# Expert stages of a hybrid layer stack: routing of the first part inside the stage ahead, and top-1 results scattered home

## The reference

```python
def _L0_ffn_ref(x, W1, b1, W2, b2, Wr, br):      # top-1: W1 (8, 128, 512), W2 (8, 512, 128)
    logits = x @ Wr + br
    idx = jnp.argmax(logits, axis=-1)
    probs = jax.nn.softmax(logits, axis=-1)
    gates = jnp.take_along_axis(probs, idx[..., None], axis=-1)[..., 0]
    ...
    for ei in range(e):
        h = jax.nn.gelu(xf @ W1[ei] + b1[ei], approximate=False)
        y = h @ W2[ei] + b2[ei]
        mask = (idxf == ei).astype(xf.dtype)
        out = out + y * (gf * mask)[:, None]

def _L1_ffn_ref(x, gate, W1, b1, W2, b2):        # top-2: W1 (8, 128, 256), W2 (8, 256, 128)
    raw_gate = jax.nn.softmax(jnp.einsum('btd,de->bte', x, gate), axis=-1)
    topk_scores, topk_idx = jax.lax.top_k(raw_gate, TOP_K)
    ...
    gate_topk = gate_topk / jnp.maximum(gate_topk.sum(axis=-1, keepdims=True), 1e-12)
    h = jax.nn.relu(jnp.einsum('btd,edh->beth', x, W1) + b1[None, :, None, :])
    expert_out = jnp.einsum('beth,ehd->betd', h, W2) + b2[None, :, None, :]
    out = jnp.einsum('bte,betd->btd', gate_topk, expert_out)
```

## Time and profile before

| | us |
|---|---|
| median of 3 runs | 2268.59 (2267.01 to 2269.56) |
| profiled execution | 2265.75 |
| its span | 2264.0 |
| stage boundaries in it | 154.1, 331.3, 847.9, 1020.5, 1167.4, 1374.6, 2060.1 |

### The profile page before, as it was taken

How to read it: one execution, slowest core, us unless ns; L and a number is a source line. 1 busy time by engine, 2 the same in 40 slices (tenths; PEclk the granted TensorE clock), 3 DMA queues, 4 the chain that set the end, 5 groups by cost and what they waited for, 6 DMA issues and landing times. The chain is left out here.

```text
span 2264.0 us, 28290 instructions
## 1 busy us (share of the span) xinstructions
PE 1647.6 (73%) x8402; PEld 974.4 (43%) x8402; DVE 1665.7 (74%) x3318; ACT 1054.8 (47%) x2009; POOL 1049.0 (46%) x845
## 2 busy tenths in 40 slices
PE   5636935899999985945635943887988888885692
PEld 2326931233333325943435941443443443343692
DVE  7985546888888825546766662899999999997664
ACT  3433640566666771626832632534434444431361
POOL 5636331222222005352207771567666666574776
PEclk8656966999999995977765976988987997896696
DMA  8012315333333201212002530000000000000363
GB/s 248 1 6 69 86 35 63 40 43 45 44 41 44 32 2 46 83 55 61 0 1 76 163 104 33 0 1 1 1 1 0 0 1 0 0 0 12 101 167 107
DMA packets 141594, 102.53 MB, mean 45 GB/s; under 512 B 16360, under 2 KB 133360, under 8 KB 141328
## 3 DMA queue, kind: packets, MB, share of 16 engines
q1 hardware_dynamic: 129168, 75.72, 15.9%
q0 software_dynamic: 12288, 25.19, 3.8%
HBM read 42.92 MB, written 38.27 MB: 36 GB/s over the span
## 5 line engine op out<-in xcount | busy, mean ns | idle before, releaser
L1520 POOL TENSOR_TENSOR m_hc<-m_state,bc 128x512 f32<-128x512 f32 x256 | 378.2, 1477 | 216.9 <-DVE m_state L1463 216.9
L931 DVE TENSOR_REDUCE maxima<-banks 128x1 f32<-128x512 f32 x512 | 320.2, 681 | 46.9 <-PE banks L781 45.8
L1390 ACT ACTIVATE banks<-banks,rates 128x512 f32<-128x512 f32 x256 | 168.8, 661 | 342.7 <-PE banks L1236 342.2
L889 ACT ACTIVATE h_p<-banks 128x512 f32<-128x512 f32 x512 | 274.0, 597 | 113.6 <-PE banks L789 112.5
L1463 DVE TENSOR_TENSOR_SCAN m_state<-banks,m_drive 128x512 f32<-128x512 f32 x256 | 310.1, 1212 | 22.9 <-ACT banks L1390 20.4
L533 POOL DMA_INDIRECT yg<-sorted_y,index x192 | 194.6, 1014 | 171.3 <-DMA sorted_y<-ys 105.3
L329 ACT ACTIVATE hid<-banks,slot 128x128 f32<-128x128 f32 x708 | 211.4, 367 | 110.1 <-PE banks L285 109.8
L522 POOL DMA_INDIRECT sorted_x<-xn,index x192 | 195.1, 1016 | 90.0 <-issue 57.1
L781 PE MATMUL banks<-ks,qs 128*128 128x512 bf16 x512 | 204.8, 402 | 40.8 <-DMA qs<-nothing 22.5
L285 PE MATMUL banks<-xt,slot 128*128 128x128 f32 x1416 | 212.4, 286 | 11.7 <-DVE slot L459 9.8
L293 PE MATMUL banks<-slot,hid 128*128 128x128 f32 x1416 | 201.1, 276 | 0.0
(11 more groups left out here) (253 smaller groups left out, 3030.6 us busy)
## 6 DMA issues: line engine op xcount, KB each, us to landing
xg<-sorted_x SPq DMA_DIRECT2D x58, 256.0 KB
sorted_y<-ys SPq DMA_DIRECT2D x58, 256.0 KB
qs<-part SPq DMA_DIRECT2D x144, 64.0 KB
ks<-part SPq DMA_DIRECT2D x144, 64.0 KB
sorted_x<-zeros SPq DMA_DIRECT2D x3, 1984.0 KB, 15.6
t1w<-in_t1w SPq DMA_DIRECT2D x16, 256.0 KB, 5.9
sorted_x<-xn,index POOLq DMA_INDIRECT x192, 2.2
yg<-sorted_y,index POOLq DMA_INDIRECT x192
```

The costliest lines, as they stand in the source:

```text
L889: act.activation(f.p[:, slot % 2, j, :], m.bank[5 + item % SHIFTED_BANKS][:, :], ACT.Exp, scale=1.0 / math.sqrt(HD)).then_inc(f.exps, 1)
L931: dve.reduce_max(f.maxima[:, tile, head:head + 1], m.bank[bank][:, :], AX_X).then_inc(f.ring_read, 1)
L1520: pool.tensor_tensor(f.hc[:, n % 8, :], f.state[:, n % 4, :], f.bc[:, now[1] % 2, 1, :], ALU.mult).then_inc(f.weighed, 1)
```

## The change

- Routing of part 0 of every expert stage is done inside the last rounds of the stage ahead, in generators that are run forward at given slots of those rounds (`front.until(...)`). It has buffers of its own (`front1...`, `front2...`). After its drain POOL scatters part 0 ahead of the barrier. DVE's slots in HEADS' last round are 0, 2, 8, 10 and 11 (statistics, normalising, choice, gates, places), in MAMBA's last full round 1, 4, 16, 20 and 26; in RWKV and LAPLACE they stand at the ends of the last rounds.
- Routing of the later parts is done inside the group loop, on PE and ACT ahead of the group that `FRONT_AT` names, on DVE two groups earlier; ranks and places are later by `RANKS_AT`. POOL's order is now [scatter(0)], rstd(1), scatter(1), rstd(2), scatter(2), then the way back.
- The top-1 stages take 3 and 5 batches. A sorted row has 129 floats, the last of them the token's number. Rows that no token fills carry a number behind the tokens'; they are written at the start by four DMAs from `pads`, which ACT fills. A result row goes home by its own number (`send_back`, one indirect DMA per group, 46 where there were 32 gathers), SP fetches each batch with a plain load, and the additions of part 0 stand six groups ahead of the loop's end. ACT's fills ahead of HEADS wait for all results kept.
- At the start POOL has two iotas more, ACT the fill of `pads` ahead of `decay`, and SP's constant loads wait for it. HEADS_GAP is 250 instead of 3392, a semaphore of HEADS is merged into another, and buffers are allocated in another order.

```diff
-PARTS = {1: (4, 4), 2: (2, 3, 3)}
+PARTS = {1: (3, 5), 2: (2, 3, 3)}
+ROW = P + 1
+EARLY_ADDS = 6
-HEADS_GAP = 3392
+HEADS_GAP = 250
+RANKS_AT = {1: 4, 2: 0}
+FRONT_AT = {1: (None, 0), 2: (None, 0, 4)}
...
+def front_vector(dve, m, f, at):
+    f.tally = Tally(dve, f.steps, f.base.steps)
+    yield at[0]
+    part_statistics(dve, m, f, f.parts[0])
+    yield at[1]
+    normalise_part(dve, m, f, 0)
+    yield at[2]
+    f.arrive(dve)
+    choose(dve, m, f, 0)
+    yield at[3]
+    gates(dve, m, f, 0)
+    yield at[4]
+    places(dve, m, f, 0)
...
 def sorted_tensor(pe, nc, m, s, f, stage):
...
     for g, (c, t) in enumerate(f.groups):
+        for p in range(1, len(f.parts)):
+            at = FRONT_AT[f.top][p]
+            if g == at:
+                pe.wait_ge(f.kept, f.base.kept + max(at - 2, 0))
+                tokens(p)
+            if g == at + RANKS_AT[f.top]:
+                pe.wait_ge(f.kept, f.base.kept + max(g - 2, 0))
+                ranks(pe, m, f, p)
...
+        if g == 0:
+            turn_sorted(0)
         if t == 0 and c + 1 < len(f.chunks):
             turn_sorted(c + 1)
         first_layer(g)
...
 def sorted_scalar(act, nc, m, s, f, stage):
...
     if f.fill:
-        act.wait_ge(f.second, f.base.second + len(f.groups))
+        act.wait_ge(f.kept, f.base.kept + len(f.groups))
...
 def sorted_vector(dve, nc, m, s, f, stage, last_stage):
...
-    statistics(f.parts[0])
-    normalise_part(0, f.parts[0])
-    for p, part in enumerate(f.parts):
-        if p + 1 < len(f.parts):
-            statistics(f.parts[p + 1])
-        route(p, part)
-        places(p, part)
-        if p + 1 < len(f.parts):
-            normalise_part(p + 1, f.parts[p + 1])
...
+    for g in range(len(f.groups)):
+        for p in range(1, len(f.parts)):
+            if g == max(FRONT_AT[K][p] - 2, 0):
+                part_statistics(dve, m, f, f.parts[p])
+                normalise_part(dve, m, f, p)
+                choose(dve, m, f, p)
+                gates(dve, m, f, p)
+            if g == max(FRONT_AT[K][p] + RANKS_AT[K] - 2, 0):
+                places(dve, m, f, p)
+        more = g + 4 < len(f.groups)
+        if more:
+            expert = expert_of(g + 4)
+        keep(g)
+        if more:
+            fill_slot(g + 4, expert)
+        if f.back and g == len(f.groups) - EARLY_ADDS:
+            add_part(f.parts[0])
...
 def sorted_pool(pool, nc, m, s, f, stage):
...
+    def send_back(g):
+        c, t = f.groups[g]
+        pool.wait_ge(f.noted, f.base.noted + c + 1)
+        pool.wait_ge(f.kept, f.base.kept + g + 1)
+        pool.indirect_dma_start(m.home[:, :], bass.IndirectOffsetOnAxis(ap=f.home[:, g:g + 1], axis=0),
+                                f.ys[:, g, :], None).then_inc(f.scattered[f.chunks[c].p], 16)
+
+    for p in range(1, len(f.parts)):
+        inverse_deviations(pool, m, f, p)
+        scatter(pool, f, p)
+    if f.back:
+        for g in range(len(f.groups)):
+            send_back(g)
...
 def sorted_sync(sp, nc, m, s, f):
...
+    def fetch(p, b):
+        sp.wait_ge(f.scattered[p], f.base.scattered[p] + 16 * (f.parts[p].lanes + f.parts[p].groups))
...
+        sp.dma_start(f.yg[:, b * TILES:(b + 1) * TILES, :], m.home[b * S:(b + 1) * S, :].rearrange("(t p) d -> p t d", p=P)).then_inc(f.stored[b % 3], 16)
...
+    front = Beside(front_vector(dve, m, f.ahead, (0, 2, 8, 10, 11)))
...
+    front = Beside(front_vector(dve, m, f.ahead, (1, 4, 16, 20, 26)))
...
-            sp.wait_ge(s.filled, 1)
+            sp.wait_ge(s.filled, 2)
...
             act.wait_ge(s.filled, 1)
+            act.activation(m.pads[:, :, 0:P], m.zeros[:, :].unsqueeze(1).to_broadcast([P, sum(back), P]), ACT.Copy).then_inc(s.filled, 1)
...
-                between(pool, n)
+                if n + 1 < len(stages) and stages[n + 1] in (TOP1, TOP2):
+                    pool.drain().then_inc(s.stage, 1)
+                    f.ahead.arrive(pool)
+                    scatter(pool, f.ahead, 0)
+                    pool.wait_ge(s.stage, 4 * (n + 1))
+                else:
+                    between(pool, n)
```

More of the change, by code:

```diff
@@ L477, in add, with add_part @@
         last.then_inc(f.added, 1)
[L479 to L497 removed]
+    def add_part(part):
         for b in part.batches:
@@ L563, in sorted_sync @@
             load(c + 3)
-        store(c)
+        if not f.back:
+            store(c)
+    if f.back:
+        for p, part in enumerate(f.parts):
+            for b in part.batches:
+                fetch(p, b)
 def experts_pool(pool, nc, m, s, f, stage):
@@ L596, in body @@
             last.then_inc(f.out, 1)
+        if now and not new:
+            pe.wait_ge(f.k_kept, BATCHES)
+            front.until(0)
+        if late and not now:
+            front.until(1)
     rounds(pe, body, 4)
@@ L637, in rwkv_vector @@
     u = f.first[:, :]
+    front = Beside(front_vector(dve, m, f.ahead, (0, 2, 3, 3, 3)))
     def body(new, now, late, done):
+        ending = late and not now
         if late:
@@ L683, in body @@
             dve.scalar_tensor_tensor(f.rw[:, :], f.num[:, :], 0.5, f.inverse[:, :], ALU.mult, ALU.mult).then_inc(f.mixed, 1)
+        if now and not new:
+            front.until(0)
+        if ending:
+            front.until(3)
     rounds(dve, body, 4)
@@ L706, in body @@
             normalise(pool, nc, m, s, ahead, stage)
+        if late and not now:
+            inverse_deviations(pool, m, f.ahead, 0)
     rounds(pool, body, 4)
@@ L853, in body @@
                 turn_maxima(now, 0)
+            if former and not now:
+                front.until(slot)
         if former:
@@ L1093, in body @@
             last.then_inc(f.out, 1)
+        if now and not new:
+            pe.wait_ge(f.queries, BATCHES)
+            pe.wait_ge(f.values_biased, BATCHES)
+            front.until(0)
+        if late and not now:
+            front.until(1)
     rounds(pe, body, 4)
@@ L1134, in laplace_vector @@
     ahead = Steps(dve, f.ahead_steps, 3)
+    front = Beside(front_vector(dve, m, f.ahead, (0, 1, 2, 2, 3)))
     def body(new, now, late, done):
+        if late and not now:
+            front.until(1)
         if done:
@@ L1189, in body @@
             dve.tensor_scalar(size, size, TINY, 8.0, ALU.max, ALU.min).then_inc(f.sizes, 1)
+        if now and not new:
+            front.until(0)
+        if late and not now:
+            front.until(2)
+        if done and not late:
+            front.until(3)
     rounds(dve, body, 4)
@@ L1393, in body @@
                 beside.until(n)
+            if now and not new:
+                front.until(n)
     rounds(act, body)
```

514 lines of the change are left out of this document (320 added, 194 removed).

## The result

| | before | after |
|---|---|---|
| median of 4 runs, us | 2267.8 (2265.82 to 2269.56) | 2338.86 (2335.64 to 2341.98) |
| profiled execution, its span | 2265.75, 2264.0 | 2340.35, 2338.2 |
| RWKV | 154.1 | 173.8 |
| first top-1 stage | 177.2 | 168.2 |
| HEADS | 516.6 | 515.4 |

The changed kernel is slower: ratio 1.0313, 95% interval 1.0295 to 1.0331. The forecast was slower, 2300 within 2275 to 2322; the time came 39 above it, outside the range.

A forecast was written before the change was run, and what follows sets the result against it. Chains of waits bound the expert stages, DVE bounds MAMBA. Top-1 stages -3.9 and -23.7, top-2 stages +29.5 each, sum +31.4 on 2265.75: 2297.2, as median 2300, range 2275 to 2322 (8 in 10).

The forecast's parts named there:

- The start, +5.3: Kernel start: ACT's pads fill ahead of decay (5.05) and POOL's two iotas (0.25) delay PE's first transposes.
- First expert matmul of the first top-1 stage, 208.1: After RWKV: routing, slot copies, statistics, power and logits put it at 202.8, with the start's 5.3 at 208.1, against 209.74.
- The top-1 loops, "+15" each: Both top-1 group loops: 4 for ranks and places, 10.2 stall for the second part's rows, 1 for additions.
- The ways back, 15.3 and 13.4: Top-1 stages, last keep to next stage: 15.3 by ACT's fills and drain, 13.4 without fills; before, 32.65 and 31.8.
- HEADS +3.3, then 28.8 to the first expert matmul: HEADS' last round: +3.3 from transposes and logits; then stage end 851.1 to first expert matmul 879.9.
- First top-2 stage with LAPLACE, +29.5: After LAPLACE: both later parts' routing and the scatter between run in sequence; last keep 1359 against 1329.65.
- 89.3 - 2.5 (the slots already filled): First top-2 stage: third to last keep takes the former 89.3, less 2.5 for slots already filled.
- MAMBA +14.0, then the last stage: DVE gets 14.0 of routing in MAMBA's last full round; last stage's last keep 2251.5 against 2222.04, +29.5 together.
- A: Rival: POOL binds the top-2 stages and starts earlier, so the kernel is faster, about 2225; chance 0.07.
- B: Rival: the top-2 stall is real but partly covered, +8 each instead of 29.5, 2257; chance 0.11.
- D: Rival: MAMBA's front places come too late for a scatter before the barrier, another +5 to +10, 2307; within forecast's 0.67.
- C: Rival: top-1 stages don't gain, second part's rows 10 later still or routing ahead costs its full 20 each, 2322; chance 0.15.

The follow-up runs named there:

- fill_first: Changed kernel with DVE's scaling of the bias row, and so its 320 KB store, after the four slot copies of the first top-1 stage: 2330.25 us, ratio 1.0287.
- no_early_adds: Changed kernel with the first part's additions behind the top-1 loop again, not six groups ahead of its end: 2327.08 us, ratio 1.0263.
- parts_4_4: Changed kernel with top-1 parts of 4 and 4 batches instead of 3 and 5, and one front slot more: 2311.36 us, ratio 1.0198.
- gathers_back: Changed kernel with top-1 stages storing sorted results and gathering them again, rows of 128 floats, no early additions: 2372.85 us, ratio 1.0468.
- no_mamba_front: Changed kernel with the last stage routing its first part itself, behind the barrier, and no routing in MAMBA: 2342.95 us, ratio 1.0341.
- rstd_first: Changed kernel with statistics of all later parts before the first kept result and POOL's powers ahead of their scatters: 2277.26 us, ratio 1.0046.
- five: Changed kernel with rstd_first, parts_4_4, pads_late, no_early_adds and fill_first together: 2249.43 us, ratio 0.9933.
- pads_late: Changed kernel with ACT's fill of pads behind decay instead of ahead of it: 2331.91 us, ratio 1.0289.
- four: Changed kernel with rstd_first, parts_4_4, pads_late and the bias row's look-up and store moved to the second top-1 stage's start: 2259.59 us, ratio 0.9966.

## Why the prediction was wrong

The direction and both mechanisms were right; the sizes were not. The two top-1 loops (21 us) and MAMBA with the last stage (17 us) make up 38 us of the miss. By its own steps, with the share of each in the 43 us by which the profiled execution missed (74.6 instead of 31.4):

- **The start, +5.3:** it was 3.8, PE's first transposes at 14.86 (ACT's fill took 5.11, as said, but not all of it reached PE), and RWKV with its routing ended 19.7 later for a forecast 20.0. Right.

```profile
14.86 0.47 PE L190 MATMUL banks<-ident,xn 128*128 128x128 f32 x1 [14.86 <-DVE w_now L1860]
```

- **First expert matmul of the first top-1 stage, 208.1:** it stood at 212.66. The step that failed is "DVE fills four slots (4)": the store of the bias row, which in the kernel before lies beside DVE's statistics, now falls into the copies and costs a gap of 7.6, of which POOL's scatters would have hidden some. +4.6; fill_first, without the gap, has the first expert matmul 34.8 after the stage's start instead of 38.9.
- **The top-1 loops, "+15" each:** +25.7 and +25.0. This is the mis-sized term with the largest share, 21 us. Ranks and places held 4, as said. The stall for the second part's rows cost 15 between two keeps (17.1, where 2 is usual) for a forecast 10.2. PE stood 12.6, since scatters were taken at 1.27 to 1.29 each, from a stretch in which DVE was routing, and took 1.47 (29.4 for 20) beside DVE's slot copies. Some 2.5 came behind it, with the granted clock at 0.50 for 4.7 us, which the working had at nothing. And "1 for the additions put into the loop" was 6: twelve additions and a batch's statistics hold the keeps for 5 us, PE has three banks and stops, and from 319.6 to 325.0 its granted clock is 0.50 again, where it is 1.00 to the loop's end in no_early_adds. no_early_adds shows that term by itself, parts_4_4 the stall.
- **The ways back, 15.3 and 13.4:** 14.7 and 12.8. Right, and gathers_back shows what they are worth.
- **HEADS +3.3, then 28.8 to the first expert matmul:** -1.2 and 29.0. Right for the second; the first part's routing in HEADS is free.
- **First top-2 stage with LAPLACE, +29.5:** +35.7. Counted from the end of the second top-1 stage, POOL's powers came within 1.2 us of where the working had them, and the second index too; the step that failed is "89.3 - 2.5 (the slots already filled)". It was 91.6, so nothing is saved by the slots. What the trace shows there: the stage's seventh keep, counted from the third, is already 1.6 later than before, PE waits 3.7 for a slot at 1266.8, and from 1268 to 1272 its granted clock is 0.57, where it was 1.00 in the same place before. No run takes the two apart.
- **MAMBA +14.0, then the last stage:** +26.2 and +20.1 for a forecast 15.5, 17 us in all. DVE's front work held it for 17.0 in place of 14.0: its windows in MAMBA's last full round add up to 16.3 (15.15 of it busy), with 0.65 of waiting ahead of the second.

```profile
2026.80:2029.20 2.40, 2.30 (x16) 1.00 0.00 0
2035.70:2038.70 3.00, 2.91 (x8) 1.00 0.00 0
2063.80:2065.20 1.40, 1.33 (x4) 1.00 0.00 0
2073.90:2078.50 4.60, 4.05 (x20) 0.87 0.00 0
2090.20:2095.10 4.90, 4.56 (x16) 0.92 0.00 0
sum 16.30, DVE 15.15; mean DVE 3.03
```

 The step that failed is that only DVE's part was counted. PE's transposes, logits and ranks and ACT's keeps stand between the steps of the scan too, and DVE, which waits for nobody in the last 32 scans of the kernel before, now waits seven times for PE or ACT, 4.3 us in all. Two of these rows, behind PE's transposes and logits, and the first early scatter, behind POOL's last product:

```profile
2056.98 0.69 DVE L1687 TENSOR_TENSOR m_drive<-banks,bc 128x512 f32<-128x512 f32 x1 [0.85 <-PE banks L1444]
...
2058.52 1.22 DVE L1693 TENSOR_TENSOR_SCAN m_state<-banks,m_drive 128x512 f32<-128x512 f32 x1 [0.86 <-ACT banks L1618]
...
2107.38 1.08 POOL L653 DMA_INDIRECT sorted_x<-front2xn,front2index  x1 [0.94 <-issue]
```

 The last 32 scans take 79.9 instead of 57.4, and no_mamba_front, which has no routing there, is back at 57.3. The mean granted clock of PE over them is 0.84 instead of 0.99; no run shows what part of the 22.5 that is. Some 4 us more arose in the rounds before; they are no effect of the change that the runs could tell: from the first scan to the 224th the other kernels took 561 to 570, the kernel before 567, and they go with the granted clock there (0.90 at 561, 0.88 or 0.89 at 564 to 568, 0.87 at 569 to 570). The last stage's part of the 17 is 4.6, 3.6 of it from the third keep to the last: 89.9 for a forecast 86.3, the same slots term again.

Of the rivals, A (POOL binds, and the early start is a gain) fell with rstd_first: POOL had as much work in that kernel and the stages were 31 and 28 shorter. B fell with the 53 us hole. D fell with POOL's first early scatter, at 2107.4, ahead of the stage's end at 2114.2. C's mechanism came in part, in the loops, on top of the forecast rather than in its place; its 2322 was the upper end of the range for that reason too low. Terms that err to the same side add up: work put into a full loop was priced by one engine's part in it alone.

By the rule in the Trainium skill (DMA: Bandwidth & Descriptors, "How a descriptor splits into AXI transactions"), a row of 516 bytes comes to at most 24 beats; the 25 in the prediction are those of its row for 576 bytes, in an estimate that the sum left out.

What is open: 5 of the 22 us that five lacks (4 of them may be those of pads_late that its trace doesn't show), 7 of the 17 that four lacks, and what the granted clock costs by itself in MAMBA and behind the top-2 holes.

## What to carry to other kernels

When work is moved, list what stands ahead of it and behind it on every in-order queue, down to the shortest instruction: a power of 2.3 us behind 24 scatters cost some 60 us in two stages, and putting it first brought the ratio from 1.0313 to 1.0046. Price a piece that is put into a full loop on all engines that do it, with what they make each other wait, and look again at what binds once a stall is gone, since the queue that was hidden behind it (here POOL's sends) ends the stage next. Early work is worth what the next wait lets it be worth: the scatter done ahead of the barrier held back the next part's power by up to 12.8 us, and putting the powers between its two halves gave 16 us. And a hole in PE's work costs more than its length, since the work behind it ran at a granted clock of 0.50 to 0.57 for 4 to 5 us.

## What the runs showed of the hardware

- A store of 320 KB whose source is one partition of SBUF (128 copies of one row) took 14 us to land. Beside it the TENSOR_LOADs with which DVE's sequencer reads an owner from SBUF took 5.3 to 7.9 us, where 0.3 is usual, and each held up its slot copy by 5.0 to 7.6 us; DVE's ordinary instructions ran on (fill_first).
- Indirect scatters of 128 rows were issued every 1.26 us beside an idle or waiting DVE, and every 1.47 to 1.55 us on average beside DVE's keeps and slot copies of 1156 columns in the top-1 loops (rows of 512 and of 516 bytes alike at 1.48).
- Behind PE's 12.6 us wait in the first top-1 loop the granted clock was 0.50 for 4.7 us with PE busy 4.6 of them; eight matmuls took 1.91 us there and 1.06 at full clock.
- Rows of 516 bytes, unaligned, were at PE 2.95 us after the issue of a load of 258 KB, against 2.78 for 256 KB in rows of 512 bytes.
